# Attention: result and shift rows turned by VectorE, wider context maxima, seven shared PSUM banks, another item order

## The chip, the cores and the metric

One Trainium2 chip, one core of it. The metric is device time of one execution in microseconds, of the compiled program from its first to its last instruction; less is better. Three executions of the kernel before are shown by their median, and one more was run under the hardware profiler, which gives the trace.

## What is computed

Eight batches of 512 tokens with 256 channels, and for each batch a context of 1601 rows with 128 channels. After a layer norm the tokens go through two attentions with shared output: a causal one over the tokens themselves, and one over the context. Both have 16 heads of 16 channels.

```python
q = _heads(x @ Wq + bq);  k = _heads(x @ Wk + bk);  v = _heads(x @ Wv + bv)
att = jnp.where(causal, jnp.einsum('bhqd,bhkd->bhqk', q, k) * scale, -jnp.inf)
y = jnp.einsum('bhqk,bhkd->bhqd', jax.nn.softmax(att, axis=-1), v)
attc = jnp.einsum('bhqd,bhkd->bhqk', qc, kc) * scale
y = y + jnp.einsum('bhqk,bhkd->bhqd', jax.nn.softmax(attc, axis=-1), vc)
```

The sum is projected, gated by tanh and added to x. A feed-forward part of two layers with six routed experts (the best two for each token) and two shared ones follows. The change touches the attention alone.

## The kernel before

The program has four stages in one launch: projections (to about 190 us of the trace), the attention (`stage_attend`, line 578), a mixing stage and the experts. The attention works on 32 **items**: one batch and four heads each (NI = 32, G = 4). The four heads stand as two pairs p with two halves h; keys and queries of a half lie on 64 partitions, of which 48 hold high and low parts of the 16 channels and two more, at rows KROWS and KROWS + 1, hold the **shift**: minus the maximum of each query's scores, as a high and a low part, so that the score matmul itself subtracts the maximum before the exponential.

For each item there are five kinds of events, and every engine goes through one list of them in one order (line 643, ORDER, a string of letters written out by hand, repeated for each item; a letter takes the next event of its kind):

- **M** (MAX): two or more matmuls make unshifted scores, and DVE reduces them to maxima. Before, 32 of them are for the context (four tiles of 402 keys, XC, for each of two p and four query tiles q), and 8 for the item's own tokens (128 to 512 keys, with four mask matmuls of 128 columns each, line 891). Lines 817 and 820 are DVE's reductions, 898 and 886 the matmuls. They are for the next item: the M letters run one item ahead.
- **H** (SHIFT): PE transposes the 16 columns of maxima (line 954), DVE writes the high and the low part (lines 834, 836), and SP moves them as four DMAs, one for each half and part, onto one partition of the queries each (line 703, `shift_rows`). Once for the context (cross) and once for the tokens (self).
- **S** (ST): a pair of score matmuls, keys on the partitions and 512 queries on the columns (line 910), each followed by an exponential on ACT into SBUF (line 867). 17 key tiles, of which tile 0 to 12 are the context and 13 to 16 the tokens; two S each. The first S of either kind waits for the shift rows (`s_shd`).
- **A** (AV): the values times half the columns of one key tile of exponentials, four heads on four groups of 32 partitions of one bank OP (line 925). A column of ones gives the denominators. The exponentials of the diagonal tiles are masked by POOL first (line 808).
- **O** (OUT): ACT copies OP to SBUF (line 875), PE transposes it in eight pieces (line 960), DVE takes the reciprocal of the denominator and multiplies (lines 841, 846), and POOL adds the two kinds (`both`, line 788); SP stores the sum as one DMA (line 708).

PSUM holds three banks for S (ST), two pairs of banks for M, H and O (R), and OP. SBUF holds three items of keys and queries; POOL splits raw keys and queries into high and low parts (lines 114, 116), some 20 us an item.

**SP's queue** is written out too. For item n: load the values of n + 2, write two blocks of zeros, self shift rows of n, load the keys of n + 3 (18 DMAs, line 680), store item n - 1, cross shift rows of n + 1, load the queries of n + 3 (12 DMAs, line 691). Each step first waits for what it moves; what stands behind a waiting step waits too.

Of the kernel before, what the change touches and what calls it, by code (L numbers as in the profile page):

```python
# [17 lines left out]
P = 128  # L18
# [5 lines left out]
G = 4  # L24
# [138 lines left out]
class First:  # L163


    def __init__(self, r_):
# [5 lines left out]
        self.part, self.mx = r_.sb("part", [P, 2, 2, QT, 4]), r_.sb("mx", [P, 2, P])  # L172
# [4 lines left out]
    def clear(self, pool):  # L177

        pool.memset(self.zero[:, :, :, :], 0.0).then_inc(self.s_fill, 1)
        pool.memset(self.mx[:, :, :], 0.0).then_inc(self.s_fill, 1)  # L180
        for h in range(2):
            pool.wait_ge(self.s_fill, h + 2)
            pool.memset(self.kraw[64 * h + 32:64 * h + 64, :, :], 1.0).then_inc(self.s_fill, 1)
        pool.wait_ge(self.s_fill, 4)
        pool.memset(self.low[:, :], 0.0).then_inc(self.s_fill, 1)
        done = 5
# [14 lines left out]
    def load_zeros(self, eng):  # L201

        eng.wait_ge(self.s_fill, 4)
# [374 lines left out]
def stage_attend(nc, a, QS, KS, VS, YS, XS, idf, idm, mqm, first, early):  # L578
# [6 lines left out]
    with ExitStack() as ctx:  # L585
        r_ = Res(nc, ctx, "at_")
        NU, NP, NB = 3, 3, 3
# [6 lines left out]
        maxima = lambda kind: mx[:, kind, 0:G * QT].rearrange("p (h r q) -> p h r q", h=2, r=2)  # L594
        sh = [r_.sb(f"sh{k}", [G * QT, 2, P], F32R) for k in range(2)]
        O = [r_.sb(f"O{k}", [P, T]) for k in range(2)]
        den = r_.sb("den", [P, 2, 2, QT * 2])
        yk = [r_.sb(f"y{k}", [P, 2, QT * 2, D]) for k in range(2)]
        ysum = [r_.sb(f"ysum{u}", [P, QT, GC]) for u in range(2)]
        ST = [r_.ps(f"ST{i}", [P, T]) for i in range(NB)]  # L600
        R = [r_.ps(f"R{i}", [P, 2, T]) for i in range(2)]
# [6 lines left out]
        (s_v, s_st, s_ex, s_msk, s_av, s_fill, s_drain, s_oe, s_ya, s_pm, s_sr, s_rc) = (  # L608
            r_.sem(n) for n in ("v", "st", "ex", "msk", "av", "fill", "drain", "oe", "ya", "pm", "sr", "rc"))
# [5 lines left out]
        FIRST, LOADS, QLOADS = 6, 6 * (len(KCUT) - 1), 12  # L615
        keys_in = lambda n: 16 * (FIRST + LOADS * n)
        XC = 402
        XOFF = [0, 400, 800, TC - XC]
        mtiles = [("x", p, q, c) for p in range(2) for q in range(QT) for c in range(4)]
        NMX = len(mtiles)  # L620
        mtiles += [("s", p, q) for p in range(2) for q in range(QT)]
# [14 lines left out]
        def halves(s):  # L636

            c0, mid = st_cols(s), T // 2
            if s < CTXT:
# [3 lines left out]
        ORDER = ("AMSMASMAMSAMSMASMAMSAMSMASMASMOSAMSMASMA"  # L643
                 "SHAMSMASMAMSAMSMASMAMSAMSMASMAMSAMSMASMA"
                 "MSAMSMAASHMASMMSAASMMSMSASMOSA")

        def take(streams, order):
# [7 lines left out]
            "S": iter([[("ST", n, s, 2 * p + h) for h in range(2)] for n in range(NI) for s in range(NKT) for p in range(2)]),  # L655
# [12 lines left out]
        slot = {e: k for k, e in enumerate(x for x in events if x[0] in ("MAX", "SHIFT", "OUT"))}  # L668

        with nc.Block() as block:  # L670

            @block.sync
            def _(sp):
# [56 lines left out]
                for n in range(NI):  # L730
# [14 lines left out]
                    if n + 1 == NI:  # L745
                        for u in range(2):
                            sp.wait_ge(s_yst[u], 16 * (NG // 2))
                        early.load(sp, a, YS)
                store(NI - 1)
                for u in range(2):  # L750
                    sp.wait_ge(s_yst[u], 16 * ((NI - u) // 2))
# [3 lines left out]
            def _(pool):  # L755
# [26 lines left out]
                rows = lambda t: t[:, :, :, :].rearrange("p h (q r) d -> p h q (r d)", q=QT)  # L782

                def both(n):
                    pool.wait_ge(s_drain, slot["OUT", n, SELF] + 1)
                    if n >= 2:
                        pool.wait_ge(s_yst[n % 2], 16 * (n // 2))
                    pool.tensor_tensor(ysum[n % 2][:, :, :].rearrange("p q (h c) -> p h q c", h=2), rows(yk[0]), rows(yk[1]),
                                       ALU.add).then_inc(s_ya, 1)
# [23 lines left out]
            def _(dve):  # L813
                def reduce_tile(n, m, k, buf):
                    if mtiles[m][0] == "s":
                        _, p, q = mtiles[m]
                        dve.tensor_reduce(maxima(SELF)[:, :, p, q], buf[:, :, 0:(q + 1) * P], AX.X, ALU.max).then_inc(s_drain, 1)  # L817
                        return
                    _, p, q, c = mtiles[m]
                    dve.tensor_reduce(part[:, :, p, q, c], buf[:, :, 0:XC], AX.X, ALU.max).then_inc(s_drain, 1)  # L820
                    if m == NMX - 1:
                        dve.wait_ge(s_drain, k + 1)
                        dve.tensor_reduce(mx[:, CROSS, 0:G * QT],
                                          part[:, :, :, :, :].rearrange("p h r q c -> p (h r q) c"), AX.X, ALU.max
                                          ).then_inc(s_pm, 1)
# [1362 lines left out]
```

## Time and profile before

| | |
|---|---|
| median of 3 runs | 2396.89 us (2394.67 to 2407.15) |
| profiled execution, span | 2442.2 us |
| own time of the profiled execution beyond its span | not given; the span is used |
| PE busy | 2327.3 us, 95% |
| DVE busy | 1848.9 us, 76% |
| ACT busy | 1558.1 us, 64% |
| POOL busy | 1080.9 us, 44% |
| mean granted TensorE clock | 0.971 |

PE is TensorE's matmuls, DVE VectorE, ACT ScalarE, POOL GpSimd, SP the engine that issues most DMAs. Busy time is the time that an engine's instructions cover. Matmuls are pipelined and the profile models their ends, so for PE the distance from one start to the next tells more than the duration. SP's DMA instructions aren't counted as busy; their lengths in the timeline are the time in which SP issues, not that in which the data moves. The granted clock is 1.00 at 2.4 GHz and 0.50 at 1.2 GHz.

### The profile page before, as it was taken

How to read it: one execution, taken by the hardware profiler on the slowest of the kernel's cores; microseconds unless marked ns; L12 is line 12 of the kernel's file. 1: busy time of each engine (PE TensorE's matmuls, PEld its weight loads, DVE VectorE, ACT ScalarE, POOL GpSimd, SP SyncE). 2: the span in 40 equal slices, each digit the busy share in tenths (PEclk: the TensorE clock that was granted, in tenths of full speed). 3: DMA queues.
4: the chain of work that ended last, by engine and by line, in shares of the span. 5: the costliest groups of instructions: out<-in, count | busy, mean ns of one | idle time of the engine just before them, and what ended most of it. 6: DMA issues, size and time to landing. Idle time of an engine off the chain costs nothing. (4 is left out here: it accounts for less than half of the span.)

```text
span 2442.2 us, 55819 instructions
## 1 busy us (share of the span) xinstructions
PE 2327.3 (95%) x20454; PEld 1492.5 (61%) x20454; DVE 1848.9 (76%) x3107; ACT 1558.1 (64%) x3328; POOL 1080.9 (44%) x663
## 2 busy tenths in 40 slices
PE   7997999999999999999999999898999989999996
PEld 7984444444444444444444444587887868878785
DVE  6768999999999999999999997375434645544647
ACT  3331888888888888888888888643344434433442
POOL 0225756564647464646565651115224153232514
PEclk9996999999999999999999999888999999999998
DMA  6998665545464546464545430542344323322623
GB/s 243 333 315 159 101 101 80 90 78 90 75 91 76 89 79 88 82 86 84 86 84 84 86 60 13 187 166 86 98 132 128 92 84 101 96 74 78 188 83 109
DMA packets 172466, 272.01 MB, mean 111 GB/s; under 512 B 48276, under 2 KB 115064, under 8 KB 170808
## 3 DMA queue, kind: packets, MB, share of 16 engines
q1 hardware_dynamic: 158856, 231.81, 42.6%
q0 software_dynamic: 12288, 33.57, 4.5%
q10 hardware_dynamic: 1072, 3.23, 0.6%
q8 instruction: 165, 2.70, 0.5%
q14 instruction: 85, 0.70, 0.1%
HBM read 165.20 MB, written 101.98 MB: 109 GB/s over the span
## 5 line engine op out<-in xcount | busy, mean ns | idle before, releaser
L867 ACT ACTIVATE at_P<-at_ST 128x512 f32<-128x512 f32 (+4 forms) x2176 | 1092.2, 558 | 233.5 <-PE at_ST L910 187.6
L820 DVE TENSOR_REDUCE f_part<-at_R 128x2 f32<-128x804 f32 x1024 | 953.4, 991 | 45.5 <-PE at_R L898 27.6
L925 PE MATMUL at_OP<-at_P,at_V 128*32 128x256 f32 x8192 | 621.7, 383 | 3.6 <-ACT at_O L875 0.8
L910 PE MATMUL at_ST<-at_Q,at_K 64*128 64x512 f32 (+4 forms) x1428 | 324.6, 428 | 0.9 <-ACT at_P L867 0.9
L925 PEld LDWEIGHTS at_OP<-at_P,at_V 128*32 128x32 f32 x8192 | 172.8, 108 | 248.7 <-ACT at_P L867 183.0
L808 POOL TENSOR_SCALAR_AFFINE_SELECT at_P<-at_P 128x512 f32<-128x512 f32 x128 | 81.5, 637 | 495.9 <-ACT at_P L867 495.9
L898 PE MATMUL at_R<-at_K,at_Q 64*128 64x402 f32 x1344 | 272.2, 401 | 2.0 <-POOL at_Q L116 2.0
L910 PEld LDWEIGHTS at_ST<-at_Q,at_K 64*128 64x128 f32 (+1 forms) x1428 | 155.1, 181 | 127.0 <-ACT at_P L867 112.4
L817 DVE TENSOR_REDUCE f_mx<-at_R 128x2 f32<-128x256 f32 (+3 forms) x256 | 204.5, 820 | 34.6 <-PE at_R L891 28.9
L1849 POOL DMA_INDIRECT ex_gb<-expert_rows,c_IDX x128 | 127.2, 993 | 231.3 <-DVE ex_ab L1906 136.9
L1056 POOL DMA_INDIRECT sorted<-c_XR,c_IDX x128 | 127.3, 994 | 227.1 <-DVE c_bcmp L1132 87.3
L1906 DVE TENSOR_TENSOR ex_ab<-ex_bank,ex_sg 128x256 f32<-128x256 f32 x148 | 62.8, 424 | 216.3 <-ACT ex_sg L1989 180.2
L898 PEld LDWEIGHTS at_R<-at_K,at_Q 64*128 64x128 f32 x1344 | 126.0, 184 | 142.8 <-DVE f_part L820 106.8
L116 POOL TENSOR_TENSOR at_K<-f_kraw,at_K 128x4226 fp32r<-128x4226 f32 x21 | 194.1, 9241 | 1.8
L1989 ACT ACTIVATE ex_sg<-ex_bank 128x256 f32<-128x256 f32 x148 | 57.0, 385 | 189.4 <-PE ex_bank L100 172.6
L910 PE MATMUL at_ST<-f_Q,f_K 64*128 64x512 f32 (+4 forms) x748 | 170.0, 430 | 0.5 <-ACT at_P L867 0.5
L898 PE MATMUL at_R<-f_K,f_Q 64*128 64x402 f32 x704 | 151.0, 425 | 8.5 <-DVE f_part L820 6.8
L98 PE MATMUL ex_bank<-c_WH,ex_xbL 128*128 x296 | 144.0, 486 | 0.0
L898 PEld LDWEIGHTS at_R<-f_K,f_Q 64*128 64x128 f32 x704 | 68.6, 192 | 87.8 <-DVE f_part L820 70.2
L910 PEld LDWEIGHTS at_ST<-f_Q,f_K 64*128 64x128 f32 (+1 forms) x748 | 80.9, 183 | 64.5 <-ACT at_P L867 61.0
L100 PE MATMUL ex_bank<-c_WH,ex_xbH 128*128 x296 | 117.9, 398 | 0.0
L99 PE MATMUL ex_bank<-c_WL,ex_xbH 128*128 x296 | 117.5, 397 | 0.0
(252 smaller groups left out, 4539.0 us busy)
## 6 DMA issues: line engine op xcount, KB each, us to landing
f_kraw<-k_rows SPq DMA_DIRECT2D x372, 88.0 KB, 5.3
f_qraw<-q_rows SPq DMA_DIRECT2D x372, 64.0 KB, 2.8
expert_rows<-ex_rb SPq DMA_DIRECT2D x148, 128.0 KB
ex_xb<-sorted SPq DMA_DIRECT2D x72, 256.0 KB
v_items<-pj_vbuf SPq DMA_DIRECT2D x8, 2176.0 KB, 8.0
f_kraw<-k_rows SPq DMA_DIRECT2D x186, 88.1 KB, 5.6
k_rows<-pj_kpart SPq DMA_DIRECT2D x16, 800.5 KB, 4.3
sorted<-f_zero SPq DMA_DIRECT2D x74, 128.0 KB, 3.9
```

Source lines behind the costliest of these rows:

```text
L98: pe.matmul(out, wL, xH, start=start, stop=False)
L99: pe.matmul(out, wH, xL, start=False, stop=False)
L100: return pe.matmul(out, wH, xH, start=False, stop=stop)
L116: pool.tensor_tensor(out, raw, out.bitcast(F32), ALU.subtract).then_inc(s_lo, 1)
L817: dve.tensor_reduce(maxima(SELF)[:, :, p, q], buf[:, :, 0:(q + 1) * P], AX.X, ALU.max).then_inc(s_drain, 1)
L820: dve.tensor_reduce(part[:, :, p, q, c], buf[:, :, 0:XC], AX.X, ALU.max).then_inc(s_drain, 1)
L867: act.activation(Pt[(NKT * n + s) % NP][0:rows, h, c0:T], ST[(NST * n + s * G + h) % NB][0:rows, c0:T], ACT.Exp, scale=SCALE).then_inc(s_e ...
L898: ins = pe.matmul(buf[:, h, 0:XC], Q[u][r0:r0 + 64, CROSS, p, q * P:(q + 1) * P], K[u][r0:r0 + 64, p, at:at + XC], start=True, stop=True)
L910: pe.matmul(ST[t % NB][0:rows, c0:T], K[n % NU][half, p, keys], Q[n % NU][half, kind, p, c0:T], start=True, stop=True).then_inc(s_st, 1)
L925: ins = pe.matmul(OP[32 * h:32 * h + 2 * D, at], V[n % 2][0:rows, key_tile(s), h, :], Pt[(NKT * n + s) % NP][0:rows, h, at], start=s in (0 ...
L1056: pool.indirect_dma_start(XS[h], bass.IndirectOffsetOnAxis(ap=self.IDX[h][:, j, t:t + 1], axis=0), XR[:, h * self.HT + t, :], None).then_i ...
L1849: pool.indirect_dma_start(gb[n % NGB][j][:, :], None, RS[h], bass.IndirectOffsetOnAxis(ap=R.IDX[h][:, j, t:t + 1], axis=0)).then_inc(s_ga[ ...
```

## The change

- **Maxima.** The context is taken in three tiles of 512 keys for each p and q, and the last 66 keys of all four q of one p together in one rest tile: 24 + 2 events M. The self maxima are five events: for each p the last query tile ("last", 512 keys) and the third and first together ("ends", 384 + 128), and the second tile of both p together ("second"). Masks are then up to 256 columns wide. An item has 31 M where it had 40.
- **Shift rows.** PE's transposes go. DVE writes the parts side by side (HL, 128 partitions x 32) and turns them by four blocks of 32 x 32 with its own transpose (hlT). A shift row then lies on four groups of partitions, and SP moves each row as four DMAs of eight pieces of 32 elements: 16 DMAs for each kind where there were four. The first S of the kind waits for all 16.
- **Result.** ACT's copy and PE's transposes go. DVE turns the bank OP (128 x 512) by blocks into SBUF (TO), once for each kind, and takes one reciprocal; POOL multiplies (512 elements) and adds. DVE waits for the last A of the kind, and the next A that writes OP waits for DVE. The store is four DMAs with pieces of 16 elements.
- **Banks.** S and M share seven banks (NB = 7); a small planner written into the kernel (`homes`) picks them from the order, and each user waits for the one before it on its bank.
- **Order.** ORDER is another string, of 101 letters instead of 110. SP's own sequence of steps is the same.

```diff
-        NU, NP, NB = 3, 3, 3
+        NU, NP, NB = 3, 3, 7
+        NSH = 16 * 2 * 2 * QT
-        ORDER = ("AMSMASMAMSAMSMASMAMSAMSMASMASMOSAMSMASMA"
-                 "SHAMSMASMAMSAMSMASMAMSAMSMASMAMSAMSMASMA"
-                 "MSAMSMAASHMASMMSAASMMSMSASMOSA")
+        ORDER = ("AOSSMAAMSMASMASMASMASMASMASMASMMSAMSAMSAMSAMSAMSAM"
+                 "SMASAHMMSAASMASMASMASMAMMSASHSMAASOMSAMSAMSSAASSMSA")
...
                 def shift_rows(n, kind):
-                    sp.wait_ge(s_drain, slot["SHIFT", n, kind] + 1)
+                    sp.wait_ge(s_sr, 2 * n + (2 if kind == SELF else 1))
                     for h in range(2):
                         for r in range(2):
-                            row = 64 * h + KROWS + r
-                            sp.dma_start(Q[n % NU][row:row + 1, kind].bitcast(F32),
-                                         sh[kind][2 * QT * h:2 * QT * (h + 1), r].bitcast(F32)).then_inc(s_shd[kind], 16)
+                            row, j = 64 * h + KROWS + r, G * QT * r + 2 * QT * h
+                            for b in range(QT):
+                                sp.dma_start(Q[n % NU][row:row + 1, kind].bitcast(F32).rearrange(
+                                                 "o p (q b i) -> o (p q) b i", b=QT, i=32)[:, :, b],
+                                             hlT[kind][32 * b + j:32 * b + j + 2 * QT, :].bitcast(F32)
+                                             ).then_inc(s_shd[kind], 16)
                 def store(n):
                     sp.wait_ge(s_ya, n + 1)
-                    sp.dma_start(YS[n // NG, :, :, n % NG * GC:(n % NG + 1) * GC], ysum[n % 2][:, :, :]).then_inc(
-                        s_yst[n % 2] if n < NI - 1 else early.s_ylast, 16)
+                    dst = YS[n // NG].rearrange("(m r) t c -> r t m c", m=QT)
+                    for h in range(G):
+                        c0 = n % NG * GC + h * D
+                        sp.dma_start(dst[:, :, :, c0:c0 + D],
+                                     ysum[n % 2][32 * h:32 * h + 32, :, :].rearrange("r (t m) d -> r t m d", m=QT)
+                                     ).then_inc(s_yst[n % 2] if n < NI - 1 else early.s_ylast, 16)
...
+                    dve.tensor_scalar(hi, t, -1.0, None, ALU.mult).then_inc(s_hl, 1)
+                    dve.wait_ge(s_hl, done + 1)
+                    dve.scalar_tensor_tensor(lo, t, -1.0, hi.bitcast(F32), ALU.mult, ALU.subtract).then_inc(s_hl, 1)
+                    dve.wait_ge(s_hl, done + 2)
                     if n >= 1:
+                        dve.wait_ge(s_shd[kind], NSH * n)
+                    dve.transpose(hlT[kind][:, :].bitcast(F32), HL[kind][:, :].bitcast(F32)).then_inc(s_sr, 1)
+
+                def output(n, kind):
+                    dve.wait_ge(s_av, av_done[n, LAST if kind == SELF else CTXT - 1])
+                    if n >= 2 and kind == CROSS:
+                        dve.wait_ge(s_ym, n - 1)
+                    t = TO[n % 2]
+                    dve.transpose(t[:, kind].rearrange("p b e -> p (b e)"), OP[:, :]).then_inc(s_oe, 1)
+                    if kind == SELF:
+                        dve.wait_ge(s_oe, 2 * (n + 1))
+                        dve.reciprocal(den[n % 2][:, :, :], t[:, :, :, D]).then_inc(s_rc, 1)
...
+                    pool.tensor_tensor(yk[:, :, :, :], TO[n % 2][:, :, :, 0:D], dk, ALU.mult).then_inc(s_ym, 1)
+                    pool.wait_ge(s_ym, n + 1)
+                    pool.tensor_tensor(ysum[n % 2][:, :, :], yk[:, 0], yk[:, 1], ALU.add).then_inc(s_ya, 1)
...
-                        pe.wait_ge(s_shd[kind], 64 * (n + 1))
+                    if p == 0 and s in (0, CTXT):
+                        pe.wait_ge(s_shd[kind], NSH * (n + 1))
```

## Rows read from the trace of the kernel before

**Rows 1.** The page's first line.
```profile
span 2442.2 us, 55819 instructions
```

**Rows 2.** Busy time by stretch: stretch, length, busy us of each engine (instructions), clock, DMA.
```profile
192.50:222.50 30.00, 21.58 (x64) 8.84 (x64) 29.18 (x33) 0.00 (x0) 10.93 (x5) 0.53 0.98 173
222.50:230.80 8.30, 7.01 (x53) 4.31 (x53) 6.19 (x10) 0.00 (x0) 8.12 (x3) 0.50 0.26 50
230.80:1535.00 1304.20, 1296.41 (x14302) 618.02 (x14301) 1193.86 (x1522) 1109.37 (x2208) 725.94 (x307) 1.00 0.50 81
```

**Rows 3.** Timeline of PE in mid attention: start, us, engine, line, out<-in, count.
```profile
818.73 0.64 PE L925 MATMUL at_OP<-at_P,at_V 128*32 128x256 f32 x8
819.30 0.50 PE L910 MATMUL at_ST<-at_Q,at_K 64*128 64x512 f32 x2
819.64 0.35 PE L898 MATMUL at_R<-f_K,f_Q 64*128 64x402 f32 x2
819.92 0.64 PE L925 MATMUL at_OP<-at_P,at_V 128*32 128x256 f32 x8
820.49 0.45 PE L898 MATMUL at_R<-f_K,f_Q 64*128 64x402 f32 x2
```

**Rows 4.** Timeline of PE while maxima alone run.
```profile
196.10 0.70 PE L898 MATMUL at_R<-f_K,f_Q 64*128 64x402 f32 x2 [0.20 <-DVE f_part L820]
197.00 0.70 PE L898 MATMUL at_R<-f_K,f_Q 64*128 64x402 f32 x2 [0.20 <-DVE f_part L820]
```

**Rows 5.** Groups by line, 800 to 1208 us: busy, mean ns | idle before.
```profile
L820 DVE TENSOR_REDUCE f_part<-at_R 128x2 f32<-128x804 f32 x316 | 294.5, 990 | 12.4 <-PE at_R L898 6.7
L817 DVE TENSOR_REDUCE f_mx<-at_R 128x2 f32<-128x1024 f32 x20 | 24.4, 1222 | 4.0 <-PE at_R L891 4.0
...
L846 DVE TENSOR_TENSOR at_y<-at_R,at_den 128x256 f32<-128x256 f32 x20 | 8.5, 425 | 0.7
...
L960 PE MATMUL at_R<-c_idf,at_O 64*128 64x64 f32 x160 | 8.8, 229 | 0.4
...
L954 PE MATMUL at_R<-c_idf,f_mx 64*128 64x64 f32 x40 | 4.4, 214 | 0.0
...
L788 POOL TENSOR_TENSOR at_ysum<-at_y 128x256 f32<-128x256 f32 x10 | 7.3, 732 | 0.8
```

**Rows 6.** Timeline of SP's DMA queue over one item.
```profile
830.28 2.67 SPq L703 DMA_DIRECT2D at_Q<-at_sh  x4
832.99 8.37 SPq L680 DMA_DIRECT2D f_kraw<-k_rows  x18
841.40 0.58 SPq L708 DMA_DIRECT2D y_rows<-at_ysum  x1
848.15 2.66 SPq L703 DMA_DIRECT2D f_Q<-at_sh  x4
850.86 5.38 SPq L691 DMA_DIRECT2D f_qraw<-q_rows  x10
```

**Rows 7.** The shift-row line: count, issue ns min/median/max, first and last start.
```profile
L703 SPq DMA_DIRECT2D at_Q<-at_sh x168: 626/629/1304, 270.3 to 1532.9; - x168
```

**Rows 8.** Timeline of SP's DMA queue: other small DMAs.
```profile
7.91 0.71 SPq L134 DMA_DIRECT2D c_graw<-in_g_ffn  x1
...
1560.80 0.28 SPq L1250 DMA_DIRECT2D mx_raw<-in_bd  x1
```

**Rows 9.** Timeline of PE around the next item's first score.
```profile
849.76 1.07 PE L925 MATMUL at_OP<-at_P,at_V 128*32 128x256 f32 x16
850.76 0.39 PE L910 MATMUL at_ST<-at_Q,at_K 64*128 64x256 f32 x2
...
853.10 0.50 PE L910 MATMUL at_ST<-f_Q,f_K 64*128 64x512 f32 x2
```

**Rows 10.** PE by stretch: busy us (instructions), clock, DMA share, GB/s.
```profile
236.00:240.00 4.00, 4.00 (x34) 0.65 1.08 113
240.00:244.00 4.00, 4.00 (x46) 1.00 1.08 120
```

More of the change, by code:

```diff
@@ L201, in load_zeros @@
     def load_zeros(self, eng):
-        eng.wait_ge(self.s_fill, 4)
+        eng.wait_ge(self.s_fill, 3)
         for n in WRITES:
@@ L593, in stage_attend @@
         zero, part, mx = first.zero, first.part, first.mx
[L594 to L601, printed above, removed]
+        HL = [r_.sb(f"HL{k}", [P, 2 * G * QT], F32R) for k in range(2)]
+        hlT = [r_.sb(f"hlT{k}", [P, 32], F32R) for k in range(2)]
+        TO = [r_.sb(f"TO{u}", [P, 2, NQB, 32]) for u in range(2)]
+        den = [r_.sb(f"den{u}", [P, 2, NQB]) for u in range(2)]
+        yk = r_.sb("yk", [P, 2, NQB, D])
+        ysum = [r_.sb(f"ysum{u}", [P, NQB, D]) for u in range(2)]
+        PS = r_.ps("PS", [P, NB, T])
         OP = r_.ps("OP", [P, T])
@@ L615, in stage_attend @@
         FIRST, LOADS, QLOADS = 6, 6 * (len(KCUT) - 1), 12
+        NSH = 16 * 2 * 2 * QT
         keys_in = lambda n: 16 * (FIRST + LOADS * n)
-        XC = 402
-        XOFF = [0, 400, 800, TC - XC]
-        mtiles = [("x", p, q, c) for p in range(2) for q in range(QT) for c in range(4)]
+        XT = TC - TC % T
+        XR = TC - XT + 1
+        mtiles = [("x", p, q, c) for p in range(2) for q in range(QT) for c in range(TC // T)]
+        mtiles += [("r", p) for p in range(2)]
         NMX = len(mtiles)
-        mtiles += [("s", p, q) for p in range(2) for q in range(QT)]
+        mtiles += [t for p in range(2) for t in (("last", p), ("ends", p))] + [("second",)]
         NM = len(mtiles)
@@ L902, in scores, with vacated @@
-                def scores(n, s, h):
+                def vacated(e, which):
+                    users = [before[e][i] for i in which if before[e][i] is not None]
+                    maxima = [slot[u] + 1 for u, _ in users if u[0] == "MAX"]
+                    exps = [NST * u[1] + u[2] * G + 2 * u[3] + h + 1 for u, h in users if u[0] == "ST"]
+                    if maxima:
+                        pe.wait_ge(s_drain, max(maxima))
+                    if exps:
+                        pe.wait_ge(s_ex, max(exps))
@@ new lines, in products, with mask @@
+                def products(n, kind, buf, at, p, q, k0, k1):
+                    u = n % NU
+                    for h in range(2):
+                        r0 = slice(64 * h, 64 * h + 64)
+                        ins = pe.matmul(buf[:, h, at:at + k1 - k0], Q[u][r0, kind, p, q * P:(q + 1) * P],
+                                        K[u][r0, p, k0:k1], start=True, stop=True)
+                    return ins
+                def mask(out, n):
+                    for j in range(2):
+                        for h in range(2):
+                            r0 = slice(64 * h, 64 * h + 64)
+                            m = mqm[r0, j:j + 1, :]
+                            ins = pe.matmul(out(h), idm[r0, j, :], bcast(m, n, 1) if n > 1 else mqm[r0, j, :],
+                                            start=False, stop=True, skip_group_check=True)
+                    return ins
@@ L908, in scores @@
-                    if t >= NB:
-                        pe.wait_ge(s_ex, t - NB + 1)
-                    pe.matmul(ST[t % NB][0:rows, c0:T], K[n % NU][half, p, keys], Q[n % NU][half, kind, p, c0:T],
-                              start=True, stop=True).then_inc(s_st, 1)
+                    for i in range(2):
+                        half = slice(64 * i, 64 * i + 64)
+                        vacated(e, (i,))
+                        pe.matmul(PS[0:rows, home[e][i], c0:T], K[n % NU][half, p, keys], Q[n % NU][half, kind, p, c0:T],
+                                  start=True, stop=True).then_inc(s_st, 1)
```

222 lines of the change are left out of this document (114 added, 108 removed).

## The prediction

> **What bounds the kernel now.** I read the page first: one profiled execution spans 2442.2 us [rows 1]. The runs shown have a median of 2396.89 us, 45 us less; I sum against the span and carry the difference over. By stretches [rows 2], the attention's steady part runs from 230.8 to 1535 us: 1304.2 us for 32 items, 40.8 us an item, with PE busy 99%, DVE 92% and ACT 85%. A busy PE need not be a limited one, so the PE timeline is next [rows 3]: a value event (A, eight matmul records) is followed by the next start 0.57 us later whatever comes next, a pair of maxima matmuls (M) by 0.28, a pair of scores (S) by 0.34. Times that repeat so exactly are streaming, not waiting. The same maxima alone, before scores begin, start every 0.90 us, paced by DVE's reduction [rows 4], and an item has 40.8/32 = 1.27 us for each of its 32 cross reductions. So PE sets the pace and DVE stands close behind. SP, which appears in no busy share, is the third to read [rows 6]: an item's queue holds four shift-row DMAs (2.67 us), 18 key loads (8.37), one store (0.58), then a pause, four shift-row DMAs again (2.66) and twelve query loads. The pause is 848.15 - 841.98 = 6.2 us, and it is what lets the second four go out the moment DVE has written the shifts.
>
> **PE.** 24 cross tiles of 512 columns replace 32 of 402. An S pair, also 512 columns, takes 0.34 and an M pair 0.28 [rows 3]: 24 x 0.34 + two rest tiles of eight 66-column products, at about 0.5 (bounds: 0.2, the columns alone at the S pair's rate, and 1.1, four M pairs) = 9.2, against 32 x 0.28 = 9.0. Self maxima keep their columns in five units; I take nothing for them, within 0.4 of a gain. The transposes leave: busy 8.8 and 4.4 us in ten items [rows 5], so at most 1.3 us an item, and from that I take 0.9, because neighbours overlap. The new order joins four pairs of A (two before); of a joined pair, 1.00 us for sixteen records [rows 9] stands against 2 x 0.57, so 0.14 each, 0.3 in all. PE gains about 1.2 us an item: 39.6.
>
> **DVE.** A reduction of 804 elements lasts 990 ns and starts every 0.90 us alone; one of 1024 lasts 1222 [rows 4, 5], so about 1.13. Cross: 24 x 1.13 + 2 x 0.6 = 28.3 against 32 x 0.90 = 28.8. The two value transposes have no row: between 425 ns (the 256-element product they replace) and 1222 (twice their elements), I take 0.7. They and the small steps on 16 and 32 elements, now four more with their waits, cost 0.5 more than the steps removed. DVE stays where it is. ACT loses two copies an item and is not the limit. POOL gains a product of 512 elements: twice the 732 ns of the 256-element sum, 1.5 us (bounds 0.7 and 3) on an engine busy 726 of 1304 us [rows 2, 5]; hidden under DMA and PE work, nothing.
>
> **SP, the term that decides.** Each shift row leaves as four DMAs instead of one: 16 for each kind instead of 4, all of which PE's first score of that kind waits for (16 x 16 counts). A shift-row DMA occupies SP 626 ns at least and 629 at the median of the 168 into one tile [rows 7] (88 more go into the other), 2.67/4 = 0.67 from start to start [rows 6]. The new form is not in the trace. Bounds: 0.33, the shortest issue that I found on SP (0.28) with its gap, and 0.75, a long small one (0.71) with its gap [rows 8]. I take 0.67: same direction, same tiles, same eight pieces and one destination partition. Sixteen then take 10.7 us. The store becomes four DMAs of the same 512 pieces each: 4 x 0.6 = 2.4 (bounds 1.3 and 3); its 64-byte pieces delay nothing, as 10.7 us of issuing follow it.
>
> What is queued behind matters as much. SP's program is unchanged: self shifts of item n, key loads of n+3, store of n-1, cross shifts of n+1, query loads. But DVE's events moved together. Before, 18 M lay between the self shift and the cross shift (848.15 - 830.28 = 17.9 us [rows 6]), longer than the 11.7 us of work that SP had between. Now 8 M lie there, some 9 us, and SP has 10.7 + 8.4 + 2.4 = 21.5 us. The cross shifts therefore start late by 12 us and take 10.7. Landing: the last of four left SP at 850.81 and the first score of the next item started at 853.10 [rows 6, 9], so 2.3 at most; I take 2.1.
>
> The loop, from the self shift being written: 21.5 + 10.7 + 2.1 = 34.3 us until PE may start the next item's first score. PE's own work over that stretch is 14 S, 12 M and 13 A, about 16 us, so it stands idle some 18 us, in two places: first at the self scores (10.7 + 2.1 = 12.8 us against 8 M, 6 S and 7 A, some 8), then, for about 14 us, at the next item's first score. From there to the next self shift PE does 20 S, 19 M and 19 A: 20 x 0.34 + 19 x 0.34 + 19 x 0.55 (0.57, joined ones 0.43) = 23.7, and DVE's small steps end some 0.3 us later: 24. Period 34.3 + 24 = **58.3 us** against 40.8.
>
> Clock: after the idle start of this stage the granted clock stood at 0.65 in one 4 us window of dense work and at 1.00 in the next [rows 10], and was 0.50 in the thin stretch before [rows 2]. Fourteen idle microseconds an item should bring that back: 4 us of work at half speed, 2 us lost. Bounds 0 and 4; I take 1.3, as I don't know that every stall does it.
>
> Sum: 29 items with key loads, 58.3 + 1.3 - 40.8 = 18.8 each, 545; two without loads, 8.4 less, 21; 12 more DMAs ahead of the first scores, 8; the last item's self wait less PE's gain, 4. Together +578: 3020 in the profile, 2397 + 578 = 2975 us for the median.
>
> **Rivals.**
> **A cheaper issue** (0.33 to 0.5). For: load issues take 0.46 [rows 6], some 0.28 [rows 8]. Against: 629 ns is almost constant over the very line that is multiplied. At 0.33 the loop is 5.3 + 8.4 + 2.4 + 5.3 + 2.1 + 24 = 47.5, +6.7 x 29 = 194, with the clock 250: 2590 to 2650. At 0.46: 27.7 + 24 = 51.7, +10.9 x 29 and small terms, with the clock 360 to 400: 2780.
>
> **Issue time that costs nothing, and a faster kernel.** PE and DVE reach the next item's first score about 15 us after the self shift. SP needs 32 issues, 2.4 of stores, 8.4 of loads and 2.1 of landing. The wait vanishes only if 32 issues fit in 15 - 12.9 = 2.1 us, 0.07 us each. Then PE's 1.2 us an item comes through: 38 us, 2355 to 2360. For it: PE is the bound now, and SP's issue lengths are known from a profiled execution alone, 45 us longer than the others. Against: no DMA on SP took under 0.28. The Trainium skill (DMA: Bandwidth & Descriptors, Issuing engines are not separate DMA queues) says that the sequencer's time to initiate a DMA is "usually small relative to the DMA itself"; by that rule this rival would win. This case's trace disagrees: 0.63 us of SP for 4 KB [rows 7]. The same page's Rules for kernel authors, that many small transfers should be joined, speak against the change.
>
> **A dearer issue**, or every stall cooling PE: at 0.75 the loop is 12 + 8.4 + 2.6 + 12 + 2.1 + 24 = 61.1, +20.3 x 29 and small terms = 630, with 2.2 us of clock 700: 3095.
>
> **The waits cancel out**: an issue just short enough that the stall eats PE's gain; 2390 to 2405.
>
> **How the numbers follow.** Forecast (issue 0.6 to 0.7) 0.60; cheaper issue 0.25; dearer 0.06; free issue, faster, 0.07; cancelling 0.02. The range runs from 2640, inside the cheaper rival, to 3080, inside the dearer one; what is left out is the faster case, the cancelling one and the outer parts of two rivals, about 0.2. A change of 0.5% (12 us) is about what a measurement of this kernel can tell from none. Slower by more: 0.91, same 0.02, faster 0.07. The likeliest case alone covers 2900 to 3040.
>
> **What would show it.** Of the changed kernel: the shift-row line on SP with 1024 issues at a median near 629 ns (right) or under 400 (the cheaper rival); SP without a pause between store and cross shifts; a PE wait on the shift-row DMA once an item, near 14 us, and a shorter one at the self scores; DVE's busy share in the attention near 65%; the granted clock under 1.00 after each stall; transposes of 128x512 near 0.7 us. It is wrong if PE remains 99% busy in this stage, or if SP waits for DVE ahead of every cross shift.

## The result, and the profile after

The changed kernel takes 3087.75 us (median of 4 runs, 3085.26 to 3092.65) against 2396.97 us, the median of four with the same kernel as before: a ratio of 1.288, 95% interval 1.285 to 1.291, so 691 us slower. Forecast were 2975 us and a range up to 3080. The sign and the place were right; the size was 113 us short. The page of the profiled execution begins:

```profile
span 3084.9 us, 54311 instructions
...
PE 2428.2 (79%) x19430; PEld 1510.2 (49%) x19430; DVE 1853.6 (60%) x2915; ACT 1517.3 (49%) x3264; POOL 1113.2 (36%) x694
```

The attention is the stretch that grew. By stretch (length, busy us of PE, PEld, DVE, ACT and POOL, clock, DMA share, GB/s):

```profile
232.00:2240.00 2008.00, 1436.59 (x13438) 655.21 (x13442) 1194.51 (x1338) 1083.93 (x2171) 757.68 (x340) 0.80 0.35 54
```

Against [rows 2] the same work lies in 2008 us instead of 1304, PE is busy 72% of it instead of 99%, DVE 59% (near 65% was forecast), and the granted clock is 0.80 instead of 1.00. The last store of the attention starts 691 us later (2245.98 against 1555.22). The stages behind it took 48 us less than in the profiled execution of the kernel before (839 against 887), which is why the spans differ by only 643.

SP's queue over one item, the answer to [rows 6] (start, us, line, out<-in, count):

```profile
1035.39 10.71 SPq L743 DMA_DIRECT2D f_Q<-at_hlT  x16
1046.15 10.04 SPq L719 DMA_DIRECT2D f_kraw<-k_rows  x18
1056.23 2.65 SPq L753 DMA_DIRECT2D y_rows<-at_ysum  x4
1058.93 12.65 SPq L743 DMA_DIRECT2D at_Q<-at_hlT  x16
1071.62 5.57 SPq L730 DMA_DIRECT2D f_qraw<-q_rows  x12
...
1100.02 10.95 SPq L743 DMA_DIRECT2D at_Q<-at_hlT  x16
```

There is no pause between the store and the second group of shift rows; the pause has moved ahead of the first group. From one self group to the next are 1100.02 - 1035.39 = 64.6 us, 64.4 on average. PE's timeline shows the two waits (the last bracket is the idle time before the row and what ended it):

```profile
1047.19 1.22 PE L997 MATMUL at_PS<-f_Q,f_K 64*128 64x512 f32 x4 [4.00 <-DMA f_Q<-at_hlT]
...
1072.64 0.79 PE L997 MATMUL at_PS<-at_Q,at_K 64*128 64x512 f32 x2 [15.00 <-DMA at_Q<-at_hlT]
```

PE stands 4.0 us at the self scores and 15.0 us at the next item's first score, both times for the shift rows. The shift-row line is as [rows 7] had it, issue ns min/median/max over the 672 into one tile:

```profile
L743 SPq DMA_DIRECT2D at_Q<-at_hlT x672: 620/629/3949, 287.6 to 2221.2; - x168
```

The median of 629 ns is the old one; the maximum isn't. The long issues have one place: the first issue behind the four stores took 1.9 to 3.9 us in each of 28 items, and those that follow, but for a few, are back near 0.63. For the item above, the same view over the first half microsecond of its second group:

```profile
L743 SPq DMA_DIRECT2D at_Q<-at_hlT x1: 2532/2532/2532, 1058.9 to 1058.9; - x1
```

The clock around the long wait, two microseconds a row (busy us of PE, instructions, clock, DMA share, GB/s):

```profile
1060.00:1062.00 2.00, 0.00 (x0) 0.93 1.41 86
1062.00:1064.00 2.00, 0.00 (x0) 0.50 0.20 15
...
1072.00:1074.00 2.00, 1.36 (x12) 0.50 0.34 98
...
1076.00:1078.00 2.00, 2.00 (x14) 0.50 0.69 143
1078.00:1080.00 2.00, 2.00 (x22) 0.80 0.97 190
1080.00:1082.00 2.00, 2.00 (x22) 1.00 0.68 236
```

The clock falls to 0.50 while PE has nothing to do, and the first five to seven microseconds of dense work after the wait run at it or partly so. The busy share of the DMA engines (the column before the last) drops from 1.41 to 0.20 just when the long first issue is over, at 1061.5. On DVE, over one item, the wide reduction and the turned result:

```profile
L868 DVE TENSOR_REDUCE f_part<-at_PS 128x2 f32<-128x1024 f32 x25 | 28.9, 1215 | 1.2 <-PE at_PS L954 1.2
...
L908 DVE STREAM_TRANSPOSE at_TO<-at_OP 128x512 f32<-128x512 f32 x2 | 1.4, 718 | 1.3 <-PE at_OP L1012 1.3
```

and on POOL, over 27 items, the product:

```profile
L834 POOL TENSOR_TENSOR at_yk<-at_TO,at_den 128x512 f32<-128x512 f32 x27 | 28.6, 1059 | 2.1
```

Turning the bank takes 0.72 us (0.7 was taken), POOL's product 1.06 us (1.5 was taken), and the wide reduction what its width says.

### The profile page after: what moved, and what is told of

It reads as the page before. It is cut to its first block and busy times, and to the rows that moved or that the text cites. A ratio compares the mean times of both kernels' runs of the same rounds, so it can differ in the third digit from the quotient of the medians.

```text
span 3084.9 us, 54311 instructions
## 1 busy us (share of the span) xinstructions
PE 2428.2 (79%) x19430; PEld 1510.2 (49%) x19430; DVE 1853.6 (60%) x2915; ACT 1517.3 (49%) x3264; POOL 1113.2 (36%) x694
## 5 line engine op out<-in xcount | busy, mean ns | idle before, releaser
L929 ACT ACTIVATE at_P<-at_PS 128x512 f32<-128x512 f32 (+4 forms) x2176 | 1085.4, 560 | 970.5 <-PE at_PS L997 919.1
L868 DVE TENSOR_REDUCE f_part<-at_PS 128x2 f32<-128x1024 f32 x768 | 887.0, 1217 | 35.5 <-PE at_PS L954 34.8
L997 PE MATMUL at_PS<-at_Q,at_K 64*128 64x512 f32 (+4 forms) x1428 | 352.7, 500 | 374.2 <-DMA at_Q<-at_hlT 374.2
L997 PEld LDWEIGHTS at_PS<-at_Q,at_K 64*128 64x128 f32 (+1 forms) x1428 | 162.3, 213 | 528.7 <-DMA at_Q<-at_hlT 386.8
L997 PE MATMUL at_PS<-f_Q,f_K 64*128 64x512 f32 (+4 forms) x748 | 183.6, 496 | 189.7 <-DMA f_Q<-at_hlT 189.4
L954 PE MATMUL at_PS<-at_K,at_Q 64*128 64x512 f32 (+3 forms) x1680 | 315.1, 418 | 5.4 <-DVE f_part L868 3.2
L954 PEld LDWEIGHTS at_PS<-at_K,at_Q 64*128 64x128 f32 x1680 | 165.2, 210 | 138.8 <-DVE f_part L868 65.9
L997 PEld LDWEIGHTS at_PS<-f_Q,f_K 64*128 64x128 f32 (+1 forms) x748 | 85.2, 210 | 269.6 <-DMA f_Q<-at_hlT 196.6
L954 PE MATMUL at_PS<-f_K,f_Q 64*128 64x512 f32 (+4 forms) x880 | 171.9, 435 | 18.4 <-DVE f_part L868 9.4
L954 PEld LDWEIGHTS at_PS<-f_K,f_Q 64*128 64x128 f32 x880 | 88.3, 215 | 94.4 <-DVE f_part L868 49.0
```

The costliest lines, as they stand in the source:

```text
L868: ins = dve.tensor_reduce(part[:, :, p, q, c], buf[:, :, :], AX.X, ALU.max)
L929: act.activation(Pt[(NKT * n + s) % NP][0:rows, h, c0:T], PS[0:rows, bank, c0:T], ACT.Exp, scale=SCALE).then_inc(s_ex, 1)
L954: ins = pe.matmul(buf[:, h, at:at + k1 - k0], Q[u][r0, kind, p, q * P:(q + 1) * P], K[u][r0, p, k0:k1], start=True, stop=True)
L997: pe.matmul(PS[0:rows, home[e][i], c0:T], K[n % NU][half, p, keys], Q[n % NU][half, kind, p, c0:T], start=True, stop=True).then_inc(s_st, 1)
```

## The experiments

Two theories stood at first. **Q**: SP issues one DMA after the other at a fixed price; 24 more an item and the key loads between the two groups set the pace. **R**: moving and landing 256 small pieces a kind costs, not issuing. A third, **B**: the new order, the shared banks or DVE's waits slow the stage by themselves. Where the expectations speak of DMAs "in the rings", they mean those that SP has issued and that are not yet moved.

**Half the DMAs, the same pieces.** Both parts of a half leave in one DMA:

```diff
-                            row, j = 64 * h + KROWS + r, G * QT * r + 2 * QT * h
+                        row, j = 64 * h + KROWS, 4 * QT * h
...
-                                sp.dma_start(Q[n % NU][row:row + 1, kind]...,
-                                             hlT[kind][32 * b + j:32 * b + j + 2 * QT, :].bitcast(F32)
+                            sp.dma_start(Q[n % NU][row:row + 2, kind]...,
+                                         hlT[kind][32 * b + j:32 * b + j + 4 * QT, :].bitcast(F32)
```

> Each shift-row DMA takes both parts of a half (16 pieces, two destination partitions): 8 DMAs a kind instead of 16, the same bytes and pieces. Theory Q (SP's issue time in series): 8 x 0.67 = 5.4 us for the self group, keys 8.9, stores 2.8, cross group 5.4 to 8, landing 1.1, PE 27.3: period 51 to 53.5 us against 64.4, so about 3090 - 29 x 12 = 2740 us (2690 to 2780). Rival R (what costs is moving and landing the 256 small pieces, not issuing): pieces unchanged, so the groups take as long as before, above 3050 us. Rival B (new order, shared banks or DVE's waits slow the stage by themselves): above 3000 us.

Measured: 2731.0 us, ratio to before 1.141 (1.137 to 1.144). SP's queue, then the line's issue times:

```profile
527.58 5.20 SPq L742 DMA_DIRECT2D at_Q<-at_hlT  x8
533.09 9.04 SPq L719 DMA_DIRECT2D f_kraw<-k_rows  x18
542.17 3.58 SPq L752 DMA_DIRECT2D y_rows<-at_ysum  x4
545.80 6.08 SPq L742 DMA_DIRECT2D f_Q<-at_hlT  x8
...
579.97 5.20 SPq L742 DMA_DIRECT2D f_Q<-at_hlT  x8
```

```profile
L742 SPq DMA_DIRECT2D at_Q<-at_hlT x336: 610/611/4002, 275.9 to 1859.9; - x168
```

A DMA with twice the pieces costs no more of SP (611 ns against 629); the first group takes 5.2 us, the second, which again stands behind the four stores, 5.6 to 8.6, and the period falls to 52.9. From eight pieces to sixteen the price stays with the DMA and doesn't follow the pieces: Q, not R.

**Another order of SP's steps**, the same DMAs:

```diff
                     shift_rows(n, SELF)
+                    if n + 1 < NI:
+                        shift_rows(n + 1, CROSS)
                     if n + 3 < NI:
...
                         load(n + 3)
                     if n >= 1:
                         store(n - 1)
-                    if n + 1 < NI:
-                        shift_rows(n + 1, CROSS)
```

> Only the order of SP's steps changes: the cross shift rows go out ahead of the key loads and the store. Theory Q: 10.8 + 10.8 + landing 1.1 = 22.7 us instead of 37, PE 27.3: period 50 us, 3090 - 29 x 14 = 2680 us (2640 to 2730); DMAs and their counts the same. If the cross group grew from 10.7 to 13.4 because keys and stores lay in the rings ahead of it, it falls back to 10.8. Rival R (small pieces land slowly): the group stays near 13 and the time above 2750. Rival B: above 3000.

Measured: 2735.07 us, ratio 1.142 (1.136 to 1.149). The cross group is back at 10.7 to 10.9 us, as expected, and most of the loss is gone with no DMA less. But the period is 52.0 us, not 50, and what PE waits for is no longer the shift rows alone: 135 us of waits over the run are for them (564 in the changed kernel), and 111 for DVE's reductions (13 there). POOL and DVE at one moment (start, us, line):

```profile
831.77 9.30 POOL L116 TENSOR_TENSOR at_K<-f_kraw,at_K 128x4226 fp32r<-128x4226 f32 x1
```

```profile
836.88 4.21 DVE L895 TENSOR_SCALAR at_HL<-f_mx 128x16 fp32r<-128x16 f32 x1
841.13 0.18 DVE L897 SCALAR_TENSOR_TENSOR at_HL<-f_mx,at_HL 128x16 fp32r<-128x16 f32 x1
```

The sign change of 16 elements, 0.17 us elsewhere, lasts 4.21 us and ends when POOL's TENSOR_TENSOR ends (831.77 + 9.30 = 841.07). The key loads now go out later, and POOL's split of the keys has moved onto DVE's shift step. The line's busy time over the run says how often: 130.7 us for 64, against 26.1 us in the changed kernel. This was not in either theory, and is taken up below.

**The store in one piece**, with the rows in another place (that layout is all that is changed of the computation):

```diff
-                    for h in range(G):
-                        c0 = n % NG * GC + h * D
-                        sp.dma_start(dst[:, :, :, c0:c0 + D], ...
+                    sp.dma_start(YS[n // NG, :, :, n % NG * GC:(n % NG + 1) * GC],
+                                 ysum[n % 2][:, :, :].rearrange("p (t m) d -> p t (m d)", m=QT)
```

> The result is stored by one DMA with pieces of 256 bytes as in the kernel before, instead of four with pieces of 64 bytes; it puts the rows in another place, so the output is not the reference's. Theory Q with the store's pieces as the cause of the grown cross group: store 0.6 instead of 2.8, cross group 10.8 to 11.5 instead of 13.4, period 64.4 - 4.5 = 60 us, about 2955 us (2930 to 2990). If the key loads in the rings are the cause: only the store's own 2.2 us go, 3020 us.

Measured: 2941.43 us, 146 less than the changed kernel; ratio to before 1.229 (1.225 to 1.232).

```profile
565.00 10.71 SPq L743 DMA_DIRECT2D at_Q<-at_hlT  x16
576.01 8.83 SPq L719 DMA_DIRECT2D f_kraw<-k_rows  x18
584.88 0.58 SPq L750 DMA_DIRECT2D y_rows<-at_ysum  x1
585.51 10.72 SPq L743 DMA_DIRECT2D f_Q<-at_hlT  x16
```

The key loads still lie in front, and the group behind them takes 10.7 us. In the changed kernel, with 2048 store pieces of 64 bytes in front as well, it takes 13.5 on average and single issues reach 3.9 us. So the form of the store, not the key loads, made SP wait; the four stores cost 2.2 us of issuing and 2.6 of what follows. The run changes two things at once, 2048 pieces to 512 and four DMAs to one, and doesn't say which of them counts. The store doesn't land later for its small pieces (6.6 us at the median, 7.6 in one DMA); that the first issue waits until part of what is queued has gone is inferred from the fall of the DMA share beside it.

**The kernel before with this one edit**: its four shift-row DMAs a kind cut into sixteen, everything else old.

```diff
+                            for b in range(QT):
-                            sp.dma_start(Q[n % NU][row:row + 1, kind].bitcast(F32),
-                                         sh[kind][2 * QT * h:2 * QT * (h + 1), r].bitcast(F32)
+                                sp.dma_start(Q[n % NU][row:row + 1, kind]....rearrange(...)[:, :, b],
+                                             sh[kind][2 * QT * h:2 * QT * (h + 1), r, 32 * b:32 * b + 32].bitcast(F32)
```

> The kernel before with one edit: each shift row goes out as four DMAs of eight pieces of 32 elements, 16 a kind. Everything else of the change is left out (PE's transposes, two R buffers, the old order). Theory Q: self group 10.8 + keys 8.4 + store 0.6 = 19.8 us, past the 17.9 us at which the cross shift is ready; then 10.8 + 1.1 = 31.7 us, and 18.6 us of PE from the first score to the next self shift, with 2 us for the clock: period 52 us against 40.8, about 2397 + 31 x 11.5 = 2750 us (2700 to 2830). Rival B: the DMAs hide behind the old order, 2397 to 2450 us.

Measured: 2757.6 us, ratio 1.152 (1.145 to 1.158), 361 us from twelve DMAs more a kind.

```profile
468.49 11.06 SPq L704 DMA_DIRECT2D at_Q<-at_sh  x16
479.61 9.23 SPq L680 DMA_DIRECT2D f_kraw<-k_rows  x18
488.88 0.58 SPq L711 DMA_DIRECT2D y_rows<-at_ysum  x1
489.51 10.74 SPq L704 DMA_DIRECT2D at_Q<-at_sh  x16
```

SP's pause between store and cross group is gone here too: 11.1 + 9.2 + 0.6 = 20.9 us of issuing now stand ahead of the cross shift rows, which DVE had ready 17.9 us after the self shift in the kernel before. The new parts of the kernel aren't needed for a loss of this kind; it is 361 us here and 691 in the change, where the order of the events has also brought the two groups together.

**The changed kernel without shift rows**: `shift_rows` returns at once, and the waits for it go. It leaves out the subtraction of the maxima.

> The changed kernel without its shift-row DMAs and without the two waits on them; the rows stay at zero, so no maximum is subtracted and the output is not the reference's. It prices all the rest of the change: order, wide maxima, shared banks, DVE's transposes, POOL's product, the four-part store. Theory Q: PE streams without a stall at some 39.6 us an item against 40.8, 2355 to 2375 us, granted clock at 1.00 in the attention. Rival B (the rest also costs): above 2410 us.

Measured: 2354.78 us, ratio 0.981 (0.977 to 0.985).

```profile
232.00:1500.00 1268.00, 1249.74 (x13330) 582.22 (x13329) 1196.93 (x1339) 1059.63 (x2149) 759.47 (x338) 1.00 0.54 85
```

Items follow each other at 40.2 us; in the kernel before at 41.3 (from POOL's copies of the values, nine items each). So all the rest of the change is worth 42 us, and B falls. (The comparison also takes away the kernel's last shift-row DMAs, four a kind before; in the kernel before, the waits of PE that the profile lists from 240 to 1500 us come to 0.2 us, so they cost it nothing to speak of.)

**Both remedies together**, eight DMAs a kind and cross shifts first:

> Both remedies in one: 8 DMAs a kind, and cross shift rows ahead of the key loads. Theory Q: self group 5.3 us, SP then waits for DVE's cross shift some 9 us after the self shift, group 5.3, landing 1.1: 15.7 us, about when PE gets to the next item's first score; stalls of 0 to 2 us, period 40 to 42 us, 2375 to 2440 us. If the miss of the order-only run (2735 where 2680 was expected) came from key and query loads that now arrive late at POOL, some of it stays here: up to 2500 us.

Measured: 2535.0 us, ratio 1.056 (1.051 to 1.062), outside both bounds. PE hardly waits for shift rows any more (0.3 us in the item looked at), but DVE's small TENSOR_SCALAR is busy 140.7 us over its 64 executions, 4 to 5 us each time that it meets POOL's key split, and PE then stands 4.4 us for DVE: 121 us over the run, against 18 in the kernel without shift rows.

**By way of DRAM**: one DMA writes the turned rows out, two bring them back, three issues instead of sixteen.

```diff
+                    sp.dma_start(SH[kind].rearrange("g b i -> b g i"), hlT[kind][:, :].bitcast(F32)).then_inc(s_pm, 16)
+                    sp.wait_ge(s_pm, 16 * (2 * n + (2 if kind == SELF else 1)))
                     for h in range(2):
+                        row = 64 * h + KROWS
+                        sp.dma_start(Q[n % NU][row:row + 2, kind].bitcast(F32),
+                                     SH[kind, 16 * h:16 * h + 16].rearrange("(r c) b i -> r (c b i)", r=2)
```

> The turned rows go to DRAM by one DMA and back by two (two destination partitions each): 3 issues a kind instead of 16, cross shift rows ahead of the key loads. Theory Q: 0.5 + 2 (write lands) + 1 + 2 = 5.5 us from shift to rows in place, within the 7 us of PE work between; no stall, 2355 to 2385 us, faster than the kernel before. Rival R (small pieces land slowly, 4 KB on few queues): stalls, above 2420 us.

Measured: 2418.38 us, ratio 1.008 (1.006 to 1.011); expected were 2355 to 2385.

```profile
810.74 0.57 SPq L742 DMA_DIRECT2D shift_rows<-at_hlT  x1
812.72 0.53 SPq L746 DMA_DIRECT2D at_Q<-shift_rows  x2
```

The way itself is no longer than expected: 0.57 us, 1.4 until the write has landed, 0.5 for two issues. What is missing lies for the most part in DVE's step (busy us, mean ns):

```profile
L899 DVE TENSOR_SCALAR at_HL<-f_mx 128x16 fp32r<-128x16 f32 x64 | 83.9, 1311 | 1.1
...
L901 DVE SCALAR_TENSOR_TENSOR at_HL<-f_mx,at_HL 128x16 fp32r<-128x16 f32 x64 | 11.2, 175 | 2.2
```

1311 ns on average instead of 175: 73 us over the run. PE waits 65 us for DVE's reductions, which stand behind this step, against 18 in the kernel without shift rows: 47 of the 63 us between the two kernels. The other 16 are not placed; the granted clock in the stage is 0.98 instead of 1.00.

**Self shift early.** One letter of ORDER moves: H from the 56th place to the second (the text below says the 54th). The count of DMAs is the change's.

> The changed kernel with one letter of ORDER moved: the self shift is the second letter instead of the 54th, since its maxima are ready by then. 16 DMAs a kind as in the change. Theory Q: self 10.8 + keys 8.9 + stores 2.8 = 22.5 us end before DVE writes the cross shift some 33 us later; only the cross group's own 10.8 + 1.1 = 11.9 us is left, against 7 us of PE work: stall about 5 us, plus some clock: period 44.5 to 46.5 us, 2355 + 31 x 6 = 2540 us (2500 to 2580). If DVE's small steps at that place meet POOL's long instructions, up to 60 more.

Measured: 2611.6 us, ratio 1.090 (1.087 to 1.093). SP and PE around the cross shift:

```profile
805.46 10.81 SPq L743 DMA_DIRECT2D f_Q<-at_hlT  x16
```

```profile
817.34 0.80 PE L997 MATMUL at_PS<-f_Q,f_K 64*128 64x512 f32 x2 [5.97 <-DMA f_Q<-at_hlT]
```

One group and its landing are left, as expected, and PE waits 6.0 us for them instead of 5; the period is 47.8, where 44.5 to 46.5 was expected. The clock was under 1.00 for 5 us on average after each wait, which costs 2.5 us of full speed, more than was allowed for. The other cause that the text names is absent: DVE's sign change is busy 16.6 us over the run and never above 0.18 in the attention's steady part.

**Both**, the DRAM route and the early self shift:

> Rows by way of DRAM (3 issues a kind), the self shift as second letter of ORDER, and SP's steps in the order of the change (keys and store ahead of the cross shift rows). Theory Q with the lock (DVE's small TENSOR_SCALAR waits out a POOL instruction that is running, seen in the first DRAM run at 1.3 us mean): POOL is done with keys and queries when the cross shift comes, and the self shift comes ahead of POOL's long ones, so the step is back at 0.17 us: 2350 to 2365 us, as fast as the kernel without shift rows (2355) and faster than the kernel before. If the lock is not the cause of the 60 us between 2418 and 2355, it stays near 2400.

Measured: 2544.31 us, ratio 1.062 (1.061 to 1.064), a miss by 180 us in the wrong direction. DVE, POOL and PE at the start of an item:

```profile
834.19 1.02 DVE L899 TENSOR_SCALAR at_HL<-f_mx 128x16 fp32r<-128x16 f32 x1
835.24 3.73 DVE L901 SCALAR_TENSOR_TENSOR at_HL<-f_mx,at_HL 128x16 fp32r<-128x16 f32 x1
```

```profile
835.16 3.79 POOL L114 TENSOR_SCALAR f_K<-f_kraw,f_low 128x4226 fp32r<-128x4226 f32 x1
```

```profile
839.96 1.94 PE L1016 MATMUL at_OP<-at_P,at_V 128*32 128x256 f32 x16 [5.14 <-DVE at_TO L912]
```

DVE's two small steps now fall just beside POOL's COPY and its TENSOR_SCALAR of 3.79 us; the second waits it out (835.16 + 3.79 = 838.95, and 835.24 + 3.73 = 838.97), the transpose of OP stands behind it, and PE stands 5.14 us for OP. Over the run PE waits 146 us for OP. The expectation had the cause right and the place wrong by a microsecond.

**The same step by another instruction**: in the first DRAM kernel the sign is turned by a reduction.

```diff
-                    dve.tensor_scalar(hi, t2, -1.0, None, ALU.mult).then_inc(s_hl, 1)
+                    dve.tensor_reduce(hi, t2.rearrange("p h (c o) -> p h c o", o=1), AX.X, ALU.max, negate=True
+                                      ).then_inc(s_hl, 1)
```

> The first DRAM kernel (2418 us) with the high part written by a negating TENSOR_REDUCE with one SBUF input instead of the TENSOR_SCALAR; the low part stays a SCALAR_TENSOR_TENSOR with two SBUF inputs. If POOL shuts out a DVE instruction by the kind of its reads, the reduction takes 0.17 us each time and the 1 to 2 us appear at the step with two inputs, the sum and the time the same (2405 to 2425 us). If any DVE instruction on SBUF is shut out, the reduction waits as the TENSOR_SCALAR did. If the wait disappears from both, the time falls to 2365 to 2390.

Measured: 2403.69 us, ratio 1.003 (1.001 to 1.005), a little under the 2405 to 2425 that were expected for the first case; PE waits 56 us for DVE's reductions instead of 65.

```profile
L902 DVE SCALAR_TENSOR_TENSOR at_HL<-f_mx,at_HL 128x16 fp32r<-128x16 f32 x64 | 76.1, 1190 | 2.2
...
L899 DVE TENSOR_REDUCE at_HL<-f_mx 128x16 fp32r<-128x16 f32 x64 | 10.5, 164 | 1.1
```

The reduction takes 164 ns on average and never more than 172, and the wait has gone to the step that reads two SBUF inputs (1190 ns; 175 in the run of 2418). In 30 of the 63 cases looked at, the reduction started while one of POOL's splits was running, so it did meet them. Whether POOL holds DVE up thus depends on the kind of instruction. The Trainium skill (SBUF — State Buffer, SBUF: two separate sides) states this: VectorE and GpSimd share one pair of ports under an exclusive lock, which a VectorE instruction takes in a two-port mode or, against a GpSimd instruction that reads SBUF, with two SBUF inputs. Its section Who interferes with whom adds that a reduction never contends on this chip and that a TENSOR_SCALAR can enter such a mode. The traces agree for the step with two inputs (1190 ns on average) and for the reduction (164). For the TENSOR_SCALAR (1311) they agree as far as it is held up; in which mode it ran, no row shows.

**A version that beats both.** The DRAM route, H as the third letter, and the low part by a reduction too: maximum and high part lie side by side, and the low part is minus their sum.

```diff
+                    two = mx[:, kind, :, :, 0, :].bitcast(F32).rearrange("p s h c -> p h c s")
...
-                    dve.scalar_tensor_tensor(lo, t2, -1.0, hi.bitcast(F32), ALU.mult, ALU.subtract).then_inc(s_hl, 1)
+                        dve.tensor_reduce(lo, two, AX.X, ALU.add, negate=True).then_inc(s_hl, 1)
```

> The DRAM route with the self shift early (third letter of ORDER, behind the transpose of the result) and both parts of the shift written by negating reductions with one input each (the low part is minus the sum of the maximum and the high part). If the 5.1 us for which PE waited in the run of 2544 us come from DVE's two-input step shut out by POOL, all three small steps now take 0.17 to 0.21 us each time, PE's wait is gone and the kernel comes to 2350 to 2370 us, 1 to 2% faster than the kernel before. Rival: the early place itself costs (PE waits for OP's transpose), then it stays above 2450 us.

Measured: 2351.22 us against 2395.81 for the kernel before, ratio 0.982 (0.981 to 0.984): 1.8% faster than the kernel before, 24% faster than the change as made. DVE's three steps, and the stretch:

```profile
L906 DVE STREAM_TRANSPOSE at_hlT<-f_mx 128x32 f32<-128x32 f32 x64 | 13.6, 212 | 2.2
L902 DVE TENSOR_REDUCE f_mx<-f_mx 128x16 fp32r<-128x32 f32 x64 | 12.0, 188 | 2.2
...
L898 DVE TENSOR_REDUCE f_mx<-f_mx 128x16 fp32r<-128x16 f32 x64 | 9.0, 141 | 1.1
```

```profile
232.00:1500.00 1268.00, 1251.90 (x13380) 578.10 (x13380) 1183.84 (x1333) 1058.58 (x2151) 757.13 (x338) 1.00 0.55 86
```

All three are at their own length, the granted clock is 1.00, and an item takes 40.0 us. PE's wait for OP is gone.

Against the run of 2544 us two things changed, the kind of both steps and their place: the transpose of OP (O) now stands ahead of them, where it stood behind. That the steps are free by their kind and not only by their place is seen where they meet POOL, here in one item's second reduction and the POOL instruction that was running:

```profile
277.57 0.19 DVE L902 TENSOR_REDUCE f_mx<-f_mx 128x16 fp32r<-128x32 f32 x1
```

```profile
277.49 3.80 POOL L114 TENSOR_SCALAR f_K<-f_kraw,f_low 128x4226 fp32r<-128x4226 f32 x1
```

The reduction starts 0.08 us after POOL's instruction and takes 0.19 us; the step with two inputs, at the same distance in the run of 2544 us, took 3.73. So it goes in 29 of the 62 cases looked at. How much of the 193 us the new place alone would have given back, no run shows.

## Why the prediction was right, and where it fell short

**Right: the bound and its replacement.** PE's streaming set the pace before; SP's queue sets it after. The issue price of 0.67 us was taken from the line multiplied, and it held (629 ns at the median). The late cross group, the two places where PE stands, the lost pause and the fallen clock are all in the trace. Halving the DMAs, reordering SP's steps and cutting up the old kernel's DMAs each moved the time by what the loop says with the lengths measured in the changed kernel, within 55 us. PE's gain was right as well, 41.3 against 40.2 without shift rows, if partly by luck: the terms of the prediction (0.9 and 0.3 gained, 0.2 lost in the context maxima) add up to 1.0 us and not to the 1.2 that it states; 1.1 was measured.

**Wrong: the size of the loop.** Predicted and measured, in us an item, from start to start and as a mean over 28 items:

| term | predicted | measured |
|---|---|---|
| self group, 16 issues | 10.7 | 10.9 |
| key loads | 8.4 | 8.9 |
| four stores | 2.4 | 2.9 |
| cross group, 16 issues | 10.7 | 13.5 |
| last issue to first score | 2.1 | 1.1 |
| first score to self shift written | 24 + 1.3 | 27.1 |
| period | 59.6 | 64.4 |

The step that failed is the sentence on the store, that "its 64-byte pieces delay nothing, as 10.7 us of issuing follow it". It asked whether the pieces would be through before the last shift row had to land, and not whether SP could go on issuing while they were still queued. It couldn't: the first shift-row issue behind them takes 1.9 to 3.9 us in every item, the group is longer than the first one by 2.6, and with the store in one DMA the growth is gone (10.7). That is 2.6 of the 4.8 us, and together with 2.2 of the stores' own issuing it is what the store experiment gave back (4.8 us an item, 146 us).

The second term mis-sized is the clock. I took 1.3 us from one example of four microseconds and doubted that every stall would bring it about. Each one does: after all 28 long waits, and after 31 of the 32 short ones, the first dense work ran at 0.50 or little more. Behind the long wait the clock is back at 1.00 after 3.5 to 6.5 us, and the shortfall adds up to 2.5 us of full speed on average (the shares missing to 1.00, summed over short stretches). Behind the short wait it costs nothing here, since PE then waits 15 us for SP anyway. In the segment behind the long wait PE needed 27.1 us where 24 were counted: 2.5 are the clock's by this estimate, 1.2 more than I took, and 0.6 stay open. The landing was overestimated by 1.0, because the four old DMAs gave only an upper bound. The key loads were taken from one item of the kernel before (8.4); over its 26 items their mean is 9.0, as after.

A loop too short by 4.8 us would make 139 us in 29 items, and the forecast was 113 short. Some 14 of the difference is the base: 40.8 us an item is the stage divided by 32, while its items follow each other at 41.3. The remaining 12 are in the small terms and not placed.

**The rivals.** The dearer issue at 3095 us came nearest in number. Its first reason, 0.75 us an issue, is not what happened: the price was as forecast and the excess came from the store's pieces. Its second, that every stall cools PE, is: it allowed 2.2 us for it, and 2.5 were measured. So 3095 is near by luck as far as the issue goes. The cheaper issue and the free one are out by the median of 629 ns. The sentence of the Trainium skill (DMA: Bandwidth & Descriptors, Issuing engines are not separate DMA queues) that an issuing engine's time is usually small beside the DMA does not hold for DMAs of 1 KB here: SP spends 0.63 us on each, and the last of a group lands within 1.1 us of its issue.

**The range** ended at 3080, 8 us under the result, and inside the rival in which every stall cools PE, which was given 0.06; what the store's pieces might do was given no bound of its own.

## What to carry to other kernels

Count the DMAs of the queue that issues them, and write its steps with their lengths beside the time at which each is needed: a queue with a pause of 6 us looks idle and may yet be the next bound, and what it has queued between two urgent steps counts as much as their own price. An engine that frees another by taking over small work needs a look at what runs beside it; the kind of the instruction can matter more than its place. Where a wait of some microseconds enters a loop that PE had filled, add the time at the lower clock behind it.

## What the runs showed that was not expected

- Sixteen pieces in a DMA take no more of SP than eight (611 and 629 ns). The price does differ by form: 423 ns at the median for a key load, 572 for the turned rows on their way to DRAM, and 243 to 246 for the DMAs that bring them back, less than the shortest issue (0.28 us) that the prediction had found. What sets it, no run shows.
- Behind four stores of 2048 pieces of 64 bytes, the next issue on SP waits, up to 3.9 us, whatever it is (a shift row in the changed kernel; with the order changed it is the query loads, 9.9 us on average for twelve instead of 5.9).
- A VectorE step on 16 elements a partition lasted up to 5 us when it met a GpSimd instruction on SBUF; the old kernel read the same values from PSUM and took at most 0.28 us, though 30 of the 63 steps looked at began beside one of POOL's splits.
